# Softmax chunk totals summed over keys by VectorE in the FFN instead of by TensorE: a transformer block on one core

## The chip, the cores and the metric

The kernel runs on one core of a Trainium2 chip. Its time is the time of one execution on the device in microseconds (us); smaller is better. The engines of the core are TensorE (PE in the rows; PEld its weight loads), VectorE (DVE), ScalarE (ACT), GpSimd (POOL) and SyncE (SP, which here only starts transfers). Each follows its own list of instructions in order, and they wait for each other by semaphores.

## The reference, cut to what matters

```python
# x (4096, 512); 16 heads of 32 dimensions; float32 throughout
q, k, v = split(x @ Wqkv, 3);  q, k = layernorm(q) * q_scale, layernorm(k) * k_scale
scores = (q / sqrt(32)) @ k.T, per head;  -inf where key > query      # causal
attn   = softmax(scores)                                             # exp / sum over keys
x = layernorm(x + (attn @ v) @ out_W)
# FFN of width 2048 with weights (int - 128) * scale
x = layernorm(x + (silu(x @ Wg.T) * (x @ Wu.T)) @ Wd.T)
```

The part that the change touches is the denominator of the softmax: for each head and query, the sum of the exponentials over all keys.

## The kernel before, in words

It has three stages: the projections with the layer norms of q and k (to about 330 us of the span), the attention (330 to 1475) and the output projection with the FFN (1475 to the end).

The attention takes the heads in four groups (`g`) of four. In a group the queries go in eight chunks (`ch`) of 512, and the keys in blocks (`kb`) of 128. A pair (chunk, key block) is a step `t`; chunk `ch` has 4(ch+1) steps, so a group has 144, and `place(t)` is a step's place in its chunk. The four key blocks on the diagonal alternate with the first full ones, so they fill places 0, 2, 4 and 6. A step does this:

- PE: `scores` makes four tiles of 128 keys x 512 queries (one per head, two heads for each unit `u`) in PSUM banks, of which there are six (`BANKS`); a tile waits until ScalarE has read the tile that was in its bank before.
- ACT: the exponential of each tile, to `probs`, a ring of six steps (`PB`). It waits until the step that had the buffer before is used up, by PE (`valued`) and by whoever adds it (`added`, `side_added`).
- POOL: `mask` sets the wrong side of a diagonal block to zero.
- PE: `weigh` multiplies the four heads' probabilities by the values, side by side in four groups of 32 columns, into one PSUM bank `ctx_acc`.
- DVE: adds the step's 128x2048 probabilities to `total[:, ch % 2]`, keys still on the partitions.

The order of PE's work is written out by `scored_before`: inside a chunk (the run) six tiles of scores, one `weigh`, six tiles, two `weigh`; near a chunk's ends (four places at its start, three at its end) four tiles and one `weigh` in turn, with one batch of eight tiles where the run ends.

The sums over keys leave DVE in three ways. In chunks 4, 5 and 6 (`QUEUED`) every fourth step is added by a transfer instead: POOL starts a DMA that accumulates the step's `probs` into `side` (12 steps a group), and DVE adds `side` to `total` once, three steps before the chunk's end (`fold_at`). Five steps a group (`pe_sums`, one in chunk 3 and four in chunk 7) are added by PE, which multiplies them by a matrix of ones into the bank `sums_acc` (L1092). And each chunk's `total` is summed over its 128 keys by PE with the same ones (`sum_total`, L852), three steps into the next chunk; DVE copies `sums_acc` out (L1195), SP stores it, and reciprocals are taken of small tiles.

`finish` is the third stage. It takes the queries again in chunks of 512; each chunk has 16 positions ("ic", i), in which PE makes gate and up for 128 of the 2048 (`gate_up`) and adds the one before to the output (`down`), ACT takes the silu, and DVE forms the product in two parts (`make_hidden`), with the norms, the residuals (`"o"`), the transposes (`"t"`) and `context` between. Buffers `xt_hi` and `xt_lo` hold the transposed input of this chunk and, from the "t" positions on, of the next.

## Time and profile before

| what | value |
|---|---|
| median of 3 runs | 2299.28 us (2298.51 to 2304.28) |
| the profiled execution's own time | 2299.23 us |
| its span, first to last instruction | 2297.4 us |
| PE busy / DVE busy / ACT busy over the span | 99% / 76% / 59% |
| granted clock of PE over the span | 0.995 |
| mean DMA rate | 108 GB/s |

The span is divided between stages with different limits, so the shares over the whole say little of one stage. In the rows, "busy" counts time covered by at least one instruction; matmuls and exponentials overlap in their pipelines, so the spacing of their starts says more than their durations.

### The profile page before, as it was taken

The numbers are of one execution on the slowest core, as the hardware profiler recorded it, in microseconds if no ns is written. First come the engines' busy times: TensorE is split into PE (matmuls) and PEld (weight loads), VectorE is DVE, ScalarE is ACT, GpSimd is POOL, SyncE is SP. The second block draws the span as 40 slices with busy tenths as digits, with TensorE's granted clock in tenths as the row PEclk, the third lists the DMA queues.
The fourth block names the chain that finished last, engine by engine and source line by source line (L and its number), as shares of the span: only waits on it lengthen the run. The fifth ranks groups of instructions, "written<-read, shape, count | busy, mean of one in ns | idle before, by whom it ended". The sixth has DMA issues, their size and how long they took to land.

```text
span 2297.4 us, 35243 instructions
## 1 busy us (share of the span) xinstructions
PE 2270.1 (99%) x12422; PEld 1423.2 (62%) x12422; DVE 1746.0 (76%) x1796; ACT 1360.0 (59%) x2790; POOL 299.0 (13%) x323
## 2 busy tenths in 40 slices
PE   9999999999999999999999999999999999999997
PEld 7888854444444444444444444488888888888886
DVE  7777769999899998989989899945655556565554
ACT  4444479999999999999999999611111111101111
POOL 2111112211112111221111211000000000000001
PEclk9999989999999999999999999999999999999999
DMA  7768893443914438144391444531102111010100
GB/s 262 260 240 283 275 245 85 123 102 79 183 39 116 104 80 176 43 110 99 82 180 43 108 108 111 193 101 36 56 19 74 38 37 47 29 56 19 37 19 20
DMA packets 133221, 247.89 MB, mean 108 GB/s; under 512 B 15256, under 2 KB 40344, under 8 KB 126880
## 3 DMA queue, kind: packets, MB, share of 16 engines
q1 hardware_dynamic: 125840, 194.72, 30.6%
q0 software_dynamic: 6912, 50.33, 9.5%
q8 instruction: 101, 1.65, 0.3%
q14 instruction: 80, 0.66, 0.1%
q10 hardware_dynamic: 288, 0.52, 0.1%
HBM read 122.83 MB, written 72.37 MB: 85 GB/s over the span
## 4 chain that ended last, share of the span: by engine, by line
PE 83%; DVE 2%; ACT 1%; issue 0%; ACTq 0%; DVEq 0%; POOL 0%; POOLq 0%
PE score L1069 25%; PE ctx_acc L1084 22%; PE slot L1502 20%; PE y L1513 10%; PE slot L1427 3%; PE sums_acc L852 1%; ACT probs L1148 1%; DVE total L1210 1%; PE sums_acc L1092 1%; PE slot L1470 1%; PE y L1427 0%; PE slot L1494 0%; DVE stats L1599 0%; DVE x_late L1744 0%; ACT ctx_out L1133 0%
## 5 line engine op out<-in xcount | busy, mean ns | idle before, releaser
L1148 ACT ACTIVATE probs<-score 128x512 f32<-128x512 f32 (+3 forms) x2304 | 1068.5, 630 | 79.6 <-PE score L1069 69.2
L1210 DVE TENSOR_TENSOR total<-total,probs 128x2048 f32<-128x2048 f32 (+3 forms) x444 | 931.5, 2098 | 84.2 <-ACT probs L1148 35.0
L1069 PEld LDWEIGHTS score<-queries,keys 98*128 98x128 f32 x2300 | 392.7, 189 | 410.3 <-ACT probs L1148 325.9
L1069 PE MATMUL score<-queries,keys 98*128 98x512 f32 (+3 forms) x2300 | 630.6, 404 | 3.3 <-ACTq L1128 3.1
L1578 ACT ACTIVATE hidden<-slot,gate_scale_sb 128x512 f32<-128x512 f32 x128 | 88.2, 689 | 631.9 <-PE slot L1502 628.5
L1084 PE MATMUL ctx_acc<-probs,values 128*32 128x512 f32 (+3 forms) x3584 | 420.9, 561 | 0.0
L1640 DVE SCALAR_TENSOR_TENSOR hidden<-slot,up_scale_sb,hidden 128x512 f32<-128x512 f32 x128 | 96.1, 751 | 252.8 <-ACT hidden L1578 252.8
L1012 POOL TENSOR_SCALAR_AFFINE_SELECT probs<-probs 128x512 f32<-128x512 f32 x128 | 178.9, 1398 | 645.2 <-ACT probs L1148 644.8
L1502 PE MATMUL slot<-xt_hi,w_front 128*128 128x512 f32 x600 | 233.6, 389 | 0.1
L1502 PE MATMUL slot<-xt_lo,w_front 128*128 128x512 f32 x600 | 233.5, 389 | 0.0
L1084 PEld LDWEIGHTS ctx_acc<-probs,values 128*32 128x32 f32 x3584 | 85.4, 108 | 186.5 <-issue 98.3
L1502 PE MATMUL slot<-xt_hi,w_back 128*128 128x512 f32 x416 | 163.2, 392 | 0.0
L1502 PE MATMUL slot<-xt_lo,w_back 128*128 128x512 f32 x416 | 162.0, 389 | 0.0
L433 PE MATMUL score<-w_hi,x_hi 128*128 128x512 f32 x384 | 156.3, 407 | 1.0 <-DVE w_lo L615 0.9
L433 PE MATMUL score<-w_hi,x_lo 128*128 128x512 f32 x384 | 150.4, 392 | 0.0
L433 PE MATMUL score<-w_lo,x_hi 128*128 128x512 f32 x384 | 149.9, 390 | 0.0
L1084 PE MATMUL ctx_acc<-probs,first_values 128*32 128x512 f32 (+3 forms) x1024 | 132.9, 591 | 0.7 <-ACT ctx_out L1133 0.7
L1389 POOL TENSOR_TENSOR rstd<-veps,minus_half 128x1 f32<-128x1 f32 x64 | 36.5, 570 | 716.2 <-DVE veps L1604 716.2
L1502 PEld LDWEIGHTS slot<-xt_hi,w_front 128*128 128x128 f32 x600 | 112.6, 188 | 23.9 <-DVE hidden L1640 0.5
L1502 PEld LDWEIGHTS slot<-xt_lo,w_front 128*128 128x128 f32 x600 | 112.6, 188 | 23.4
L1513 PE MATMUL y<-w_front,h_hi 128*128 128x512 f32 x288 | 112.0, 389 | 0.0
L1513 PE MATMUL y<-w_front,h_lo 128*128 128x512 f32 x288 | 112.0, 389 | 0.0
(152 smaller groups left out, 2252.3 us busy)
## 6 DMA issues: line engine op xcount, KB each, us to landing
side<-probs POOLq DMA_DIRECT2D x48, 1024.0 KB, 6.9
queries<-q_hi SPq DMA_DIRECT2D x64, 256.0 KB
keys<-k_hi SPq DMA_DIRECT2D x64, 256.0 KB
wq_int<-in_wq SPq DMA_DIRECT2D x48, 256.0 KB, 3.3
wq_float<-wq_f SPq DMA_DIRECT2D x48, 256.0 KB, 2.9
x_raw<-in_x_t SPq DMA_DIRECT2D x32, 256.0 KB, 4.2
k_lo<-part_lo SPq DMA_DIRECT2D x32, 256.0 KB, 2.4
queries<-q_lo SPq DMA_DIRECT2D x32, 256.0 KB
```

What stands on the lines that cost most here:

```text
L433: ins = pe.matmul(bank[:], x[:, par, dc, rows], w[:, dc, m * D:(m + 1) * D], start=dc == 0 and a == 0, stop=dc == DC - 1 and a == 2)
L1012: pool.affine_select(out=view, in_=view, compare_op=ALU.is_ge, fill=0.0, base=0, pattern=[[0, HG], [1, P]], channel_multiplier=-1).then_in ...
L1069: pe.matmul(bank(v)[:, cut(t):], keys[0:ROWS, kb // ST, h, kb % ST * P:(kb % ST + 1) * P], queries[0:ROWS, q_buffer[ch], h, cut(t):], star ...
L1084: ins = pe.matmul(ctx[h * HD:(h + 1) * HD, n0:], value(kb)[:, h * HD:(h + 1) * HD], probs[:, t % PB, h, n0:], start=t in first, stop=t in ...
L1148: act.activation(probs[:, t % PB, h, cut(t):], bank(v)[:, cut(t):], ACT.Exp).then_inc(exped, 1)
L1210: dve.tensor_tensor(into, into, now, ALU.add).then_inc(added, 1)
L1389: pool.tensor_tensor(rstd[:, k, st:st + 1], veps[:, k, st:st + 1], minus_half[:], ALU.pow).then_inc(rooted[k], 1)
L1427: ins = pe.matmul(bank[:], a[:, h, g, q * P:(q + 1) * P], w[:, g, :], start=first, stop=g == NG - 1 and a is cp_lo)
L1502: ins = pe.matmul(slot[pos % 2][q][:], v(w[:, dc * P:(dc + 1) * P]), v(x[:, par, dc, :]), start=dc == 0 and a == 0, stop=dc == DC - 1 and ...
L1513: ins = pe.matmul(y[st][:], v(x[:, st * P:(st + 1) * P]), v(tile(i, 2)), start=i == 0 and a == 0, stop=i == IC - 1 and a == 1)
L1578: act.activation(hidden[:, i % 2, :], slot[pos % 2][0][:], ACT.Silu, scale=gate_scale[:, i:i + 1]).then_inc(gated, 1)
L1640: dve.scalar_tensor_tensor(hid, slot[pos % 2][1][:], up_scale[:, i:i + 1], hid, ALU.mult, ALU.mult)\
```

## The change

- No sums on PE: `sum_total`, the five `pe_sums` steps, the bank `sums_acc`, DVE's `take_sums` and the small stores and reciprocals are gone.
- `QUEUED` is now (3, 4, 5, 6, 7): 2 + 3 + 4 + 5 + 6 = 20 steps a group go by accumulating transfer, into two side buffers (`sides`, by the chunk's parity), and 124 steps by DVE.
- DVE's fold is gone. POOL starts a transfer instead that accumulates `total` into the side buffer (`fold`), four steps into the next chunk.
- Each chunk's totals, 1 MB a chunk and group (128 keys x 4 heads x 512 queries), are stored to DRAM by SP (`store_total`), from `total` for chunks 0 to 2 and from the side buffer for chunks 3 to 7; chunk 0's twice.
- The sum over keys is made later by DVE: the totals come back with the queries on the partitions (`piece_load`, runs of 256 bytes) and `tensor_reduce` sums over keys. For chunks 0 and 1 this is done in the last group of the attention, 16 pieces of 16 keys (512 KB each), one every five steps from step 46; for chunks 2 to 7 (and an unused copy of chunk 0) in the FFN, four pieces of 32 keys (1 MB each) for each of seven chunks.
- The freed PSUM bank is a seventh bank of scores.
- SP's transfers are issued in an order written out by steps; three of the next group's eight key loads now start inside chunk 7.

```diff
-    BANKS = 6
-    PE_SUMS = 5
-    QUEUED = (4, 5, 6)
+    BANKS = 7
+    QUEUED = (3, 4, 5, 6, 7)
+    FOLD_LAG, SIDE_LAG = 4, 8
+    PIECE_FROM, PIECE_EVERY, PIECE_LAG = 6, 5, 3
...
+    piece_at = [first[QUEUED[1]] + PIECE_FROM + PIECE_EVERY * p for p in range(2 * PIECES)]
...
-                if by_pe(t):
...
-                        ins = pe.matmul(sums[h * HD:(h + 1) * HD, n0:], ones[:], probs[:, t % PB, h, n0:],
-                                        start=opens, stop=False)
...
-                    if t - TOTAL_LAG in last:
-                        sum_total(pe, g, last.index(t - TOTAL_LAG))
...
+        def wait_total_free(engine, g, ch):
+
+            if ch >= 2:
+                before, gb = ch - 2, g
+            else:
+                before, gb = NCH + ch - 2, g - 1
+            if gb < 0:
+                return
+            if before in QUEUED:
+                engine.wait_ge(folded, 16 * (NF * gb + folds_before(before) + 1))
+            else:
+                engine.wait_ge(total_stored[ch % 2], total_stores(gb, before))
...
+            def fold(g, ch):
+
+                pool.wait_ge(added, NA * g + adds_before(last[ch] + 1) + A_CREDIT)
+                pool.wait_ge(side_added, 16 * (NQ * g + queued_before(last[ch])))
...
+                pool.dma_start(sides[ch % 2][:], total[:, ch % 2, :, :], accum_op=ALU.add).then_inc(folded, 16)
...
                         elif place(t) == 1:
 
 
-                            dve.wait_ge(totaled, NCH * g + ch + 1)
+                            wait_total_free(dve, g, ch)
...
-                    if t in fold_at:
-                        dve.wait_ge(side_added, 16 * (NQ * g + queued_before(last[ch])))
...
+                    if g == NG - 1 and t in piece_at:
+                        reduce_piece(piece_at.index(t))
...
+            def reduce_piece(n, par, p):
+
+                dve.wait_ge(piece_in[p % 2], 16 * NG * (LATE_PIECES // 2 * n + p // 2 + 1))
+                dve.tensor_reduce(part[:, p, :], piece_room(1 - par, p).rearrange("p k q -> p q k"), AX.X, ALU.add).then_inc(reduced, 1)
...
+                        reduce_in = (5, 6, 11, 12) if before else (1, 2, 11, 12)
+                        if after and i in reduce_in:
+                            reduce_piece(n, par, reduce_in.index(i))
```

Where instructions stand before and after, at the three places that matter:

PE in the first group before: the one step of chunk 3 that goes to the sums (731), the batch of eight tiles where that chunk's run ends (736), and the sum of chunk 3's total after the third step of chunk 4 (746):

```order
730 L1084 MATMUL ctx_acc<-probs,values 32x512 x4
731 L1092 MATMUL sums_acc<-probs,ones 32x512 x4
732 L1069 MATMUL score<-queries,keys 128x512 x6
...
736 L1069 MATMUL score<-queries,keys 128x512 x8
737 L1084 MATMUL ctx_acc<-probs,values 32x512 x4
...
745 L1084 MATMUL ctx_acc<-probs,values 32x384 x4
746 L852 MATMUL sums_acc<-total,ones 32x512 x4
747 L1069 MATMUL score<-queries,keys 128x128 x4
```

and the end of chunk 3 after (the tiles of a batch stand in several rows, since the seventh bank has a name of its own):

```order
727 L1135 MATMUL score<-queries,keys 128x512 x3
728 L1135 MATMUL score_spare<-queries,keys 128x512
729 L1135 MATMUL score<-queries,keys 128x512 x6
730 L1150 MATMUL ctx_acc<-probs,values 32x512 x4
...
742 L1150 MATMUL ctx_acc<-probs,values 32x384 x4
743 L1135 MATMUL score<-queries,keys 128x128 x4
```

Both groups of `sums_acc` are gone and nothing else of PE's has moved; the batch at the run's end is in three rows.

POOL after, from chunk 7 of the first group over the start of the second (AFFINE_SELECT is `mask`; x5 is the four steps of chunk 0 and the first of chunk 1):

```order
59 L1078 DMA side_odd<-probs 128x2048 [waits side_stored1,exped]
60 L1063 AFFINE_SELECT probs<-probs 128x4x128 [waits exped]
61 L1080 DMA side_odd<-probs 128x2048 [waits side_added,exped] x5
62 L1063 AFFINE_SELECT probs<-probs 128x4x128 [waits exped] x5
63 L1089 DMA side_odd<-total 128x2048 [waits folded,added,side_added]
64 L1063 AFFINE_SELECT probs<-probs 128x4x128 [waits exped] x10
```

and DVE's adds at the start of the second group after (chunk 0, then chunk 1 from the third row on):

```order
394 L1275 TENSOR_TENSOR total<-probs 128x4x384 [waits masked,folded,exped]
395 L1270 TENSOR_TENSOR total<-total,probs 128x4x256 [waits added,masked,exped]
396 L1270 TENSOR_TENSOR total<-total,probs 128x4x128 [waits added,masked,exped]
397 L1275 TENSOR_TENSOR total<-probs 128x2048 [waits masked,folded,exped]
398 L1270 TENSOR_TENSOR total<-total,probs 128x4x384 [waits added,masked,exped]
```

The first add of chunk 1 (397) needs the buffer that chunk 7 used, and so the transfer of POOL's row 63; before, it waited for `sum_total`.

SP after, in the last group, in chunk 6 (L144 stores the product of chunk 5, L941 its side buffer, L151 loads a piece):

```order
747 L144 DMA ctx<-ctx_out 128x512 [waits ctx_taken]
748 L151 DMA piece<-totals 32x16x64 [waits reduced]
749 L151 DMA piece<-totals 32x16x64 x3
750 L941 DMA totals<-side_odd 128x2048 [waits folded]
751 L151 DMA piece<-totals 32x16x64 [waits reduced]
752 L151 DMA piece<-totals 32x16x64 x3
```

The piece that DVE needs at place 12 of the chunk (751) stands in line behind the side buffer's store (750), which waits for POOL's fold; it is so in chunks 4, 5 and 6. Before, this line held neither.

## Rows read from the trace of the kernel before

**Rows 1.** The page: each engine's busy time, its share of the span, and instructions.
```profile
PE 2270.1 (99%) x12422; PEld 1423.2 (62%) x12422; DVE 1746.0 (76%) x1796; ACT 1360.0 (59%) x2790; POOL 299.0 (13%) x323
```
**Rows 2.** Stretches (second group, last group, FFN): length, busy us, clock, DMA share.
```profile
618.00:907.00 289.00, 288.73 (x1833) 127.45 (x1832) 263.77 (x133) 269.90 (x585) 53.09 (x44) 1.00 0.47 104
...
1196.00:1475.00 279.00, 278.37 (x1764) 121.78 (x1762) 256.91 (x127) 259.55 (x558) 50.13 (x39) 1.00 0.42 109
...
1560.00:2200.00 640.00, 639.94 (x2870) 528.84 (x2870) 365.58 (x644) 98.36 (x156) 27.39 (x50) 1.00 0.13 39
```
**Rows 3.** The page's chain that ended last, by engine and line.
```profile
PE score L1069 25%; PE ctx_acc L1084 22%; PE slot L1502 20%; PE y L1513 10%; PE slot L1427 3%; PE sums_acc L852 1%; ACT probs L1148 1%; DVE total L1210 1%; PE sums_acc L1092 1%; PE slot L1470 1%; PE y L1427 0%; PE slot L1494 0%; DVE stats L1599 0%; DVE x_late L1744 0%; ACT ctx_out L1133 0%
```
**Rows 4.** Waits from 330 to 1500: us in total, times, longest.
```profile
ACT probs L1148 <- PE score L1069: 65.5, 85, 1.4
...
ACT probs L1148 <- DVE total L1210: 3.1, 2, 1.7
```
**Rows 5.** Timeline of PE in chunk 7's run: start, us, what.
```profile
852.08 1.06 PE L1084 MATMUL ctx_acc<-probs,values 128*32 128x512 f32 x8
853.07 1.66 PE L1069 MATMUL score<-queries,keys 98*128 98x512 f32 x6
...
864.13 1.06 PE L1084 MATMUL ctx_acc<-probs,values 128*32 128x512 f32 x8
865.01 1.04 PE L1092 MATMUL sums_acc<-probs,ones 128*32 128x512 f32 x8
865.98 0.50 PE L1069 MATMUL score<-queries,keys 98*128 98x512 f32 x1
```
**Rows 6.** Timeline of PE where the run of chunk 6 ends.
```profile
824.03 1.66 PE L1069 MATMUL score<-queries,keys 98*128 98x512 f32 x6
825.62 1.07 PE L1084 MATMUL ctx_acc<-probs,values 128*32 128x512 f32 x8
826.62 2.52 PE L1069 MATMUL score<-queries,keys 98*128 98x512 f32 x8
829.07 1.06 PE L1084 MATMUL ctx_acc<-probs,values 128*32 128x512 f32 x8
```
**Rows 7.** Timeline of ACT in the same run.
```profile
799.67 32.63 ACT L1148 ACTIVATE probs<-score 128x512 f32<-128x512 f32 x65
```
**Rows 8.** Instructions of DVE by shape, second group: busy us, mean ns | idle before.
```profile
L1210 DVE TENSOR_TENSOR total<-total,probs 128x2048 f32<-128x2048 f32 x88 | 204.5, 2324 | 16.0 <-ACT probs L1148 8.0
...
L1195 DVE COPY sums_out<-sums_acc 128x512 f32<-128x512 f32 x8 | 5.5, 684 | 2.1 <-PE sums_acc L852 2.1
```
**Rows 9.** Instructions of DVE by shape, 0 to 330: reductions.
```profile
L659 DVE TENSOR_REDUCE whole<-wq_f 128x512 f32 x36 | 24.4, 676 | 0.0
```
**Rows 10.** The tile `side`: POOL's issues, and its transfers' time to landing.
```profile
L1028 POOL DMA_DIRECT2D side<-probs x36: 838/855/907, 415.6 to 1394.9; - x36
...
DMA to landing us min/median/max: 4.4/6.9/8.7
```
**Rows 11.** DMA issues: count, KB each, median us to landing.
```profile
w_front<-wq_float SPq DMA_DIRECT2D x7, 1024.0 KB, 5.7
...
x_late<-sums SPq DMA_DIRECT2D x1, 224.0 KB, 2.8
```
**Rows 12.** Timelines of POOL and ACT where the third group starts.
```profile
903.57 0.63 POOL L1012 TENSOR_SCALAR_AFFINE_SELECT probs<-probs 128x512 f32<-128x512 f32 x1 [1.96 <-ACT probs L1148]
...
913.54 0.78 ACT L1148 ACTIVATE probs<-score 128x128 f32<-128x128 f32 x4 [0.54 <-PE score L1069]
```
**Rows 13.** Timelines of DVE and ACT where the attention ends.
```profile
1461.12 14.27 DVE L1210 TENSOR_TENSOR total<-total,probs 128x2048 f32<-128x2048 f32 x6
...
1461.83 10.56 ACT L1148 ACTIVATE probs<-score 128x512 f32<-128x512 f32 x21
```
**Rows 14.** Timeline of DVE in the FFN, positions 6 and 12 of a chunk.
```profile
1630.33 0.75 DVE L1640 SCALAR_TENSOR_TENSOR hidden<-slot,up_scale_sb,hidden 128x512 f32<-128x512 f32 x1 [3.04 <-ACT hidden L1578]
...
1674.18 0.75 DVE L1640 SCALAR_TENSOR_TENSOR hidden<-slot,up_scale_sb,hidden 128x512 f32<-128x512 f32 x1 [2.58 <-ACT hidden L1578]
```

More of the change, by code:

```diff
@@ L843, in attend, with bank @@
         g_full = probs[:, 0, 2, 0:P]
-        def sum_total(pe, g, ch):
-            opens = not any(by_pe(x) for x in range(first[ch], last[ch] + 1))
-            if opens:
-                pe.wait_ge(sums_taken, NCH * g + ch + 1)
-            pe.wait_ge(added, NA * g + adds_before(last[ch] + 1) + A_CREDIT)
-            for h in range(HG):
-                ins = pe.matmul(sums[h * HD:(h + 1) * HD, :], ones[:], total[:, ch % 2, h, :], start=opens, stop=True)
-            ins.then_inc(totaled, 1)
-        def bank(v):
-            return score[v % BANKS // 2][:, v % 2, :]
+        def bank(g, v):
+            b = (HG * NS * g + v) % BANKS
+            return spare if b == BANKS - 1 else score[b // 2][:, b % 2, :]
+        def wait_total_free(engine, g, ch):
[9 more added lines that the diff above has]
+                engine.wait_ge(total_stored[ch % 2], total_stores(gb, before))
         def value(kb):
@@ L1085, in weigh, with group @@
                                     probs[:, t % PB, h, n0:], start=t in first, stop=t in last)
[L1086 to L1093 removed]
                 ins.then_inc(valued, 1)
[L1096 removed]
+            def group(g, after):
                 done = early
```

371 lines of the change are left out of this document (213 added, 158 removed).

## The prediction

> **What bounds the kernel now.** I read the page first, then tables by stretch, and then the chain, the waits and timelines inside a group. The page has PE busy for 99% of the span and the other engines much less [rows 1], and the chain of work that ended last is PE's in attention and FFN alike, with the sums at 1% and 1% [rows 3]. By stretch the picture splits. In the FFN PE is busy for 639.94 of 640 us and DVE for 365.58. In an attention group of 289 us, though, ACT is busy for 269.9 and DVE for 263.8 [rows 2]: three engines within 10%, so work taken from PE pays only until the next one is in the way.
>
> "Busy" covers overlapping matmuls, so the question is what PE waits for. In the run, PE's pattern takes three steps: a lone `weigh` starts at 852.08 and the one of the pattern after next at 864.13, so a pattern takes 6.02 us [rows 5]. ACT does 65 exponentials in 32.63 us without a gap that the view shows, 0.502 each, which is also 6.02 us for twelve [rows 7]. Two engines at one pace: one follows. All ACT waits in the attention come to 65.5 us for PE's scores and 3.1 for DVE [rows 4]. ACT waits for PE and next to nothing else, so PE leads. The 65.5 us is also a ceiling: PE can become faster by about that before ACT stands in its place.
>
> **The sums on PE.** Per group of four heads: eight `sum_total` and five steps, 13; in four groups 52. One costs this: `weigh` to the next score is 853.07 - 852.08 = 0.99 us; with the sums between it is 865.98 - 864.13 = 1.85 [rows 5]. Net 0.86. The last two (the step 143 of the last group, and chunk 7's total) stand behind the last `weigh`, where the head of the next stage waits for DVE anyway, so 50 count: 50 x 0.86 = 43.0 us. Nothing hides them; each moves PE's next scores, for which ACT waits. Of the 65.5 us they use two thirds. **-43.0**.
>
> **The seventh bank.** In the run six tiles take 825.62 - 824.03 = 1.59 us, so eight at that pace would take 2.12; the batch of eight took 829.07 - 826.62 = 2.45 [rows 6]. So 0.33 us is lost where tiles seven and eight wait for ACT to free a bank. One more bank lets PE go on one exponential (0.502) earlier, which covers it. Chunks 2 to 7 have such an end: 24 in all, 0 to 24 x 0.33 = 8 us. Batches of six never need the seventh. I take 0.3 each, since ACT may be what bounds the steps just behind. **-7**.
>
> **DVE's adds.** Per group three adds, three folds and eight copies go: 6 x 2.3 + 5.5 = 19.3 us of DVE's 263.8 [rows 2, 8]. That is room, not time; DVE held ACT up for 3.1 us in all.
>
> **The head.** Six adds without a gap end at 1475.39, when ACT had been done since 1472.39 [rows 13], and the next stage's first work on DVE stands behind them. Step 143 was PE's; now DVE has one add more, 2.3 us, partly made up since its backlog at step 138 is smaller. **+1.5** (0 to 2.4).
>
> **The fold at a group's start.** The first add of chunk 1 used to wait for `sum_total`; now it waits for POOL's transfer of chunk 7's total, issued after the mask of chunk 1's first step. That mask ends at 903.57 + 0.63 = 904.20. With landings as those of `side`, 6.9 us from the issue [rows 10, 12], the total is free at 911.1, the add (2.3) ends at 913.4. Behind it ACT waits: step 10 writes the buffer of step 4, which it did at 913.54 [rows 12], and by 912.7 once the sums between are gone. So 0.7 us is lost without contention. But SP stores chunk 0's total at that time, twice (2 MB; 1 MB took 5.7 us to land [rows 11]), on the same DMA engines: up to 5 us more. It happens three times: 0 to 3 x 6 = 18. I take 2.5 each, nearer to the row without contention. **+7.5**.
>
> **The pieces in the last group.** 16 reductions of 16 x 64 = 1024 elements: a reduction of 512 takes 0.676 [rows 9], so one of 1024 about 1.2, 19 us together, and some 2 for the rest. DVE in that group: 256.9 - 19.3 + 21 = 258.6 of 279 - 11 = 268 [rows 2]: 96%, and in the runs of chunks 4 to 7 nearly all, since three adds in four steps are 3 x 2.36 = 7.1 and a piece every five steps adds 1.0 per four, together the 8.03 that four steps take. No room for late pieces there, and three are late: SP may issue them only behind the side buffer's store, which waits for the fold (issued after place 4, landed 6.9 us later, at place 8 to 9); then 1 MB (5.7) and 512 KB in runs of 256 bytes (224 KB took 2.8 us, so 6.4 at most [rows 11]) land at place 11.5 to 14, for use at 11 or 12. DVE stalls 2 to 4 us each, which ACT feels where its six buffers are used up. **+6** (0 to 25).
>
> A rule of the Trainium skill bears on how such transfers share the engines. Each DMA engine, it says, takes turns between queues at whole packets of some 9 to 17 descriptors (DMA: Bandwidth & Descriptors, section on queues, rings and completion order). By it an accumulating transfer would hold back a piece for its whole length, and pieces would land at the late end; by [rows 10, 11] alone they could as well share. No row here has the two together. The sum by the rule would be some 5 us larger.
>
> **More transfers.** 20 steps a group go by transfer in place of 12, and five folds; the time to landing must stay below what six buffers give. A buffer comes back five steps (10.0 us) after its exponentials; POOL's issue is 0.86 and landing 6.9, 8.7 at worst [rows 10]: up to 9.6. Key loads now run beside them in chunk 7, so I take **+1** (0 to 10).
>
> **The FFN.** Four reductions of 2048 elements a chunk, each (by 0.676 for 512, less a fixed part) about 2.3 us, and a small end. They stand behind `make_hidden` at positions 5, 6, 11, 12, where DVE then idles for 3.04 and 2.58 us [rows 14] (and more at 6 and 12). They fit, the tightest by 0.3. The pieces (2 MB, 6 x 2 x 2 = 24 us at the most by the same row) have five positions of 5.4 us and more. DMA share there is 0.13 [rows 2]. **0**.
>
> Sum: -43.0 - 7 + 1.5 + 7.5 + 6 + 1 = -34.0. The profiled execution took 2299.23 us, 1.8 more than its span and the same as the median of the runs. 2299.2 - 34.0 = **2265 us**.
>
> **The rivals.** (a) *All is hidden*: the fold does not collide, pieces are in time, the bank gives its 8: 2299 - 43 - 8 + 1 = 2249. For it: DVE's fresh room and a mean DMA share of 0.47. (b) *DVE becomes the bound where it reduces*: the reductions read with a step of 64 elements, which no instruction in this trace does. If they take twice the row's price, the last group gets 17 us more on an engine with 9 free, +8 to the sum above, and in the FFN 4.6 us against idle of 3.04 and 2.58 leaves some 2 us a chunk, 7 x 2 = 14: 2287. The Trainium skill speaks for it: SBUF is read in lines of 16 bytes, and strides that leave the line at each element pay a penalty (SBUF — State Buffer, under the DMA port swizzle); it gives no price. (c) *ACT takes over*: PE and ACT have the same 6.02 us pace, and if ACT's own limit is near that, only what lies at the chunks' edges is gained: 32 x 0.86 = 27 less the losses of 16: 2288. Against it: exponentials at 0.502 include the waits in [rows 4]. (d) *The side transfers are late*, the one that ends slower: an aside that lands 9.2 us or more after its issue holds ACT at the buffer. There are 80 of them; 0.5 us each is 40 and cancels the gain, 1 us each gives 2299 - 34 + 80 = 2345. It decides from a mean landing of 9.7 us, 2.8 over today's; the longest now is 8.7.
>
> **How the numbers follow.** A measurement of this kernel can tell 0.3%, 7 us, from no change. Forecast (2256 to 2276) 0.42; (a) 0.20; (b) 0.13; (c) 0.12; (d) 0.07, half of it slower than before by more than 7 us; other mixtures 0.06, on the slow side of 2276 and half of them within 7 us. The range 2246 to 2290 leaves out (d), most mixtures and the ends of (a). Faster: 0.91; same 0.04; slower 0.05.
>
> **What would show it.** A group of 278 to 281 us instead of 289; run pattern still 6.02 us (if less, PE was following ACT: (c) in reverse); batches of eight at 2.1. DVE's first add of chunk 1 waiting for a DMA for 5 us or more, and ACT for that add, three times; waits of DVE for pieces at place 11 or 12 only in the last group. (b) shows in the duration of the reductions, (d) in `side` landing above 9 us and ACT waiting for a DMA. PE must stay busy for all of 1560 to 2160; any wait of gate and up for `make_hidden` refutes my zero.

## The result and the profile after

| | before | after |
|---|---|---|
| median, us | 2299.11 (4 runs, 2298.51 to 2304.28) | 2382.14 (4 runs, 2374.78 to 2382.79) |
| ratio of the medians | | 1.0349, 95% interval 1.0323 to 1.0374 |
| span of the profiled execution | 2297.4 us | 2381.0 us |
| granted clock over the span | 0.995 | 0.971 |

The change makes the kernel 3.5% slower. The forecast was 1.5% faster, and its range (2246 to 2290) missed. In what follows, a side transfer is one of POOL's accumulating transfers of a step's `probs` into a side buffer (1 MB). These are lines of the page of the kernel after, the engines and then the two DMA queues that matter (q1 is fed by SyncE, q0 by POOL's side transfers and folds):

```profile
PE 2276.3 (96%) x12006; PEld 1422.7 (60%) x12006; DVE 1814.5 (76%) x1797; ACT 1357.1 (57%) x2789; POOL 337.7 (14%) x375
...
q1 hardware_dynamic: 279360, 269.74, 44.9%
q0 software_dynamic: 14400, 104.86, 19.8%
```

PE was busy for 99% [rows 1] and is for 96% of a longer span: it now waits for something. Stretches, columns as in [rows 2]:

```profile
330.00:400.00 70.00, 50.35 (x320) 22.48 (x318) 41.91 (x22) 45.27 (x107) 13.70 (x12) 0.83 0.74 189
700.00:1000.00 300.00, 289.62 (x1751) 127.56 (x1750) 250.55 (x120) 270.84 (x590) 64.09 (x58) 0.97 0.73 177
1300.00:1560.00 260.00, 231.13 (x1282) 97.54 (x1281) 223.41 (x115) 205.92 (x431) 42.40 (x41) 0.94 0.84 192
1660.00:2285.00 625.00, 624.12 (x2792) 514.40 (x2791) 452.98 (x667) 98.04 (x156) 26.41 (x48) 1.00 0.46 82
```

In the attention the transfer engines' share rose from 0.42 to 0.47 to 0.73 to 0.84, and no compute engine fills these stretches. In the FFN PE is still busy throughout. The waits from 330 to 1560 (total, times, longest) name the new owners:

```profile
ACT probs L1201 <- PE score L1135: 46.2, 48, 3.0
ACT probs L1201 <- DMA side_odd<-probs: 34.5, 10, 6.7
ACT probs L1201 <- DVE total L1275: 32.9, 4, 21.1
DVE total L1275 <- DMA side_odd<-total: 26.4, 3, 9.1
DVE total L1275 <- DMA totals<-total: 24.9, 1, 24.9
DVE part L1248 <- DMA piece<-totals: 23.8, 6, 7.0
```

Beside [rows 4]: the wait for PE's scores fell from 65.5 to 46.2 (50.4 with the seventh bank's tiles, which have a name of their own), as forecast; the other five lines are waits for transfers, or ACT's for a DVE add that had waited for one.

**Where the time is.** ACT copies each chunk's result out once, so the spacing of these copies is a chunk's duration. Of the second group's chunk 7, after and before:

```profile
857.91 0.78 ACT L1186 ACTIVATE ctx_out<-ctx_acc 128x512 f32<-128x512 f32 x1
931.45 0.69 ACT L1186 ACTIVATE ctx_out<-ctx_acc 128x512 f32<-128x512 f32 x1
```
```profile
832.11 0.68 ACT L1133 ACTIVATE ctx_out<-ctx_acc 128x512 f32<-128x512 f32 x1
899.01 0.60 ACT L1133 ACTIVATE ctx_out<-ctx_acc 128x512 f32<-128x512 f32 x1 [1.04 <-PE sums_acc L1092]
```

73.5 us against 66.9. All chunks of the profiled execution, read in this way (us; g0 to g3 are the groups, the last column is chunk 0 of the next group):

| | ch1 | ch2 | ch3 | ch4 | ch5 | ch6 | ch7 | ch0 |
|---|---|---|---|---|---|---|---|---|
| before, each group (last: ch7 64.2) | 15.4 | 23.6 | 32.5 | 39.6 | 47.8 | 55.8 | 66.9 | 7.6 |
| after, g0 | 14.4 | **44.9** | 30.8 | 41.4 | 49.7 | 54.4 | **72.5** | 7.3 |
| after, g1 | **19.8** | 22.5 | 31.2 | 39.4 | 46.7 | 55.2 | **73.5** | 7.3 |
| after, g2 | **20.7** | 22.5 | 31.7 | 38.3 | 46.5 | 54.4 | **73.4** | 7.3 |
| after, g3 | **19.9** | 22.5 | 31.1 | **43.3** | **54.2** | **63.0** | **86.0** | |
| undisturbed (the best seen) | 14.4 | 22.5 | 31.0 | 38.3 | 46.5 | 54.4 | 61.9 | 7.3 |

From the last copy to the end: 823.0 before, 827.5 after. The last row (its 61.9 is from e3 below) sums to 276.3 against 289.2: the wanted gain is there where nothing disturbs, 12.9 us a group, some 51 in all, against my 43 + 7. What outweighs it, counted against the undisturbed row: g0's chunk 2, 22.4; chunk 1 of g1 to g3, 17.2; chunk 7 of g0 to g2, 33.7; chunks 4 to 6 of g3, 21.3; its chunk 7, 26.8 (against 64.2 - 5.0); the end, 4.5; small ones, about 9. Together 135 less 51 is 84, the difference of the spans.

### The profile page after: what moved, and what is told of

It is laid out like the page before. It is cut to its first block and busy times, and to the rows that moved or that the text cites. A ratio compares the mean times of both kernels' runs of the same rounds, so it can differ in the third digit from the quotient of the medians.

```text
span 2381.0 us, 34948 instructions
## 1 busy us (share of the span) xinstructions
PE 2276.3 (96%) x12006; PEld 1422.7 (60%) x12006; DVE 1814.5 (76%) x1797; ACT 1357.1 (57%) x2789; POOL 337.7 (14%) x375
## 3 DMA queue, kind: packets, MB, share of 16 engines
q1 hardware_dynamic: 279360, 269.74, 44.9%
q0 software_dynamic: 14400, 104.86, 19.8%
## 5 line engine op out<-in xcount | busy, mean ns | idle before, releaser
L1201 ACT ACTIVATE probs<-score 128x512 f32<-128x512 f32 (+3 forms) x1975 | 980.1, 667 | 149.3 <-PE score L1135 44.1
L1270 DVE TENSOR_TENSOR total<-total,probs 128x2048 f32<-128x2048 f32 (+3 forms) x432 | 906.9, 2099 | 132.4 <-ACT probs L1201 85.8
L1135 PE MATMUL score<-queries,keys 98*128 98x512 f32 (+3 forms) x1971 | 601.9, 411 | 66.7 <-ACT probs L1201 63.6
L1135 PEld LDWEIGHTS score<-queries,keys 98*128 98x128 f32 x1971 | 350.2, 193 | 434.3 <-ACT probs L1201 361.9
L1150 PE MATMUL ctx_acc<-probs,values 128*32 128x512 f32 (+3 forms) x3584 | 435.1, 578 | 7.9 <-ACT ctx_out L1186 4.6
L1201 ACT ACTIVATE probs<-score_spare 128x512 f32<-128x512 f32 (+3 forms) x329 | 221.0, 672 | 14.3 <-PE score_spare L1135 5.6
L1150 PE MATMUL ctx_acc<-probs,first_values 128*32 128x512 f32 (+3 forms) x1024 | 138.0, 612 | 1.8 <-POOL probs L1063 1.8
L1135 PE MATMUL score_spare<-queries,keys 98*128 98x512 f32 (+3 forms) x329 | 135.9, 413 | 3.7 <-ACT probs L1201 3.6
```

The lines of the kernel that those rows point to most:

```text
L1135: pe.matmul(bank(g, v)[:, cut(t):], keys[0:ROWS, kb // ST, h, kb % ST * P:(kb % ST + 1) * P], queries[0:ROWS, q_buffer[ch], h, cut(t):], s ...
L1150: ins = pe.matmul(ctx[h * HD:(h + 1) * HD, n0:], value(kb)[:, h * HD:(h + 1) * HD], probs[:, t % PB, h, n0:], start=t in first, stop=t in ...
L1201: act.activation(probs[:, t % PB, h, cut(t):], bank(g, v)[:, cut(t):], ACT.Exp).then_inc(exped, 1)
L1270: dve.tensor_tensor(into, into, now, ALU.add).then_inc(added, 1)
```

## The experiments

Each ran with the kernel before on the same chip (2298.9 to 2301.9). "After" is 2382.1, and its own four executions lie 8 us apart, so a difference of a few us from it shows little by itself; there the chunks of the profile say where it lies.

**e1: the first loads spread.** In group 0, one load of keys and values goes ahead and the others stepwise, as in the later groups.

```diff
-            for j in range(AHEAD, NCH):
-                load_kv(0, j)
+            load_kv(0, AHEAD)
...
-                    if g and at == 3 and ch in (1, 2, 3):
+                    if at == 3 and ch in (1, 2, 3):
...
-                    if g and at == 7 and ch == 2:
+                    if at == 7 and ch == 2:
```

> Edit: in group 0 the key and value loads of chunks 4 to 7 are issued step by step as in the other groups, not all at once ahead of everything. Theory T (named transfers come late because of what stands ahead of them at that place): the store of chunk 0's totals is no longer behind 5 MB of loads, DVE's one wait of 24.9 us for it goes, chunk 2 of group 0 takes 23 us instead of 44.9, total 2382 - 21 = 2361 (2355 to 2366). Rival U (the DMA engines as a whole are too full, share 0.73 against 0.47, and any relief is lost again elsewhere): 2373 or more. Rival C (the stall costs most through TensorE's clock, which falls to 0.5 after it): 2350 or less, since the low-clock stretch behind the stall goes too.

2358.8, ratio 1.0256 (1.0239 to 1.0273), 23.3 less; g0's chunk 2 took 22.5, and chunks 3 and 4, where loads now run, 3.3 and 1.0 more. The time is in theory T's range. The stall in the kernel after, from a timeline of SP, DVE and ACT:

```profile
343.97 1.08 SPq L99 DMA_DIRECT2D values<-v_rows  x1
...
352.67 1.99 SPq L947 DMA_DIRECT2D totals<-total  x2
...
367.23 2.29 DVE L1275 TENSOR_TENSOR total<-probs 128x2048 f32<-128x2048 f32 x1 [24.86 <-DMA totals<-total]
369.60 0.79 ACT L1201 ACTIVATE probs<-score 128x128 f32<-128x128 f32 x4 [21.06 <-DVE total L1275]
```

Chunk 2's first add needs the buffer whose total is being stored. SP comes to the store only behind five loads, at 352.67, and it lands 14 us later behind their data. I had weighed this wait for chunks 7 to 1, where a fold holds the buffer, and never for chunks 0 to 2, where a store does.

**e2: the fold earlier**, at step 1 of the next group instead of 4.

```diff
-                    elif g and t == FOLD_LAG:
+                    elif g and t == 1:
```

> Edit: at a group's start GpSimd issues the fold of chunk 7 behind step 1's mask instead of step 4's. Theory T: it lands three steps (5.7 us) sooner, DVE's three waits of 9 us before the first add of chunk 1 fall to about 3, chunk 1 takes 15 to 16 us instead of 20, total 2382 - 13 = 2369 (2364 to 2374). Rival U: the fold meets the key and query loads of the group's start and lands as late as before, 2378 or more.

2373.75, 1.0322 (1.0304 to 1.0339), 8.4 less; chunk 1 took 17.7, 16.3 and 18.0. At the slow end of the theory: of the 17.2 us over the undisturbed chunk, half went with the earlier issue. DVE's three waits for the fold still came to 19.6 us, 6.8 at most, in place of 26.4; that the other transfers there are what keeps them long is argued, not shown.

**e3: without the next group's first loads in chunk 7.**

```diff
+                if g and j < AHEAD:
+                    sp.sem_inc(k_in[j], 48)
+                    sp.wait_ge(valued, NS * g + end + V_CREDIT)
+                    sp.sem_inc(v_in[j], 16)
+                    return
                 key_load(sp, dr, keep, g, j, k_in[j])
```

> Leaves out: the key and value loads of the next group's first three chunks (1 MB each, issued inside chunk 7), so groups 1 to 3 compute on group 0's keys there. Theory T: the accumulating transfers of chunk 7 start late because of these loads; without them chunk 7 of groups 0 to 2 takes 62 to 64 us instead of 73, total 2382 - 30 = 2352 (2345 to 2360), and side transfers land in about 7 us with none over 9. Rival U: the engines stay at a share above 0.65 and chunk 7 stays above 69 us, 2372 or more.

2345.3, 1.0208 (1.019 to 1.0225), 36.8 less, the largest single piece. Chunk 7 took 62.7, 61.9, 61.9, and ACT's wait for side transfers fell from 34.5 us to this (with the other buffer's, from 37.0 to 13.9):

```profile
ACT probs L1206 <- DMA side_odd<-probs: 8.3, 5, 3.2
```

In the kernel after, the place looks like this (POOL and SP in the second group's chunk 7):

```profile
883.51 0.65 SPq L76 DMA_DIRECT2D keys<-k_hi  x1
886.40 0.85 POOL L1080 DMA_DIRECT2D side_odd<-probs  x1 [12.06 <-DMA side_odd<-probs]
...
899.97 0.84 POOL L1080 DMA_DIRECT2D side_odd<-probs  x1 [12.71 <-DMA side_odd<-probs]
```

POOL waits 12 us for the side transfer before it may issue the next. The view of the tile gives 13.0 us from the issue at 886.40 to the landing, and 7.2 for the one at 899.97, beside which no load is issued. Undisturbed, two side transfers are issued four steps apart, 8.0 us; as each waits for the one before, a landing later than that also delays the next.

**e4 and e5: the pieces.** e4 leaves out loads and reductions of chunks 0 and 1 in the last group, e5 the reductions alone.

```diff
# e4
-                piece_load(sp, dr, piece[:], n, slice(k * PIECE_KEYS, (k + 1) * PIECE_KEYS), piece_in)
+                sp.sem_inc(piece_in, 16 * NG)
# e4, e5
-                dve.tensor_reduce(part[:, k, :], piece[:].rearrange("p k q -> p q k"), AX.X, ALU.add).then_inc(reduced, 1)
+                dve.sem_inc(reduced, 1)
```

> Leaves out: the sum over keys of chunks 0 and 1 in the last group, both the 16 loads of 512 KB in runs of 256 bytes and VectorE's 16 reductions (the inverses of these chunks are stored as ones). Theory T: chunks 4 to 7 of the last group take what they take in groups 1 and 2, or less where those have key loads: 39, 47, 55 and 64 us instead of 43, 54, 63 and 86, total 2382 - 41 = 2341 (2333 to 2350). Rival U: 20 us or more of that loss stays, from the accumulating transfers and weight loads alone, 2360 or more.

> Leaves out the 16 reductions of the pieces of chunks 0 and 1 in the last group (and the small sum and reciprocal behind them; ones are stored as their inverses), but keeps all loads of the pieces and DVE's waits for them. Theory D (VectorE's time is the cost: 16 reductions of 1.99 us and the small ones, about 34 us, on an engine that has about 9 us free in that group): the time is near that of the kernel that leaves out loads and reductions, 2350 to 2360. Rival Q (the transfers are the cost: 8 MB of pieces in runs of 256 bytes beside the side transfers, which then land late): most of the 29 us stays, 2370 to 2380.

e4: 2353.4, 1.0238 (1.0221 to 1.0255), 28.8 less, where 41 was expected; chunks 4 to 7 of the last group took 39.4, 50.2, 54.4, 76.7. e5: 2366.45, 1.0292 (1.0274 to 1.0311), 15.7 less; 41.7, 52.6, 59.0, 77.9. Neither pure theory: DVE's time is 16 us and the loads 13. And chunk 7 stays 17.5 us over the undisturbed 59.2 without any piece, so something else disturbs it.

**e10: the same reductions, read in order.**

```diff
-piece[:].rearrange("p k q -> p q k")
+piece[:].rearrange("p k q -> p (k q)").rearrange("p (q k) -> p q k", q=QB)
```

> The 16 reductions of 1024 elements in the last group and the 28 of 2048 in the FFN read the same tiles and as many elements, but in runs of neighbouring elements, so that they sum the wrong ones; loads and waits are unchanged. Theory S (the step of 64 elements between reads is what doubles the reduction's time): 1024 elements take 1.15 to 1.25 us in place of 1.99 and 2048 take 2.3 to 2.4 in place of 3.8; VectorE gets 13 us back in the last group and the time comes down by 5 to 10 us there and up to 3 in the FFN: 2370 to 2378. Rival (a reduction is this slow for its count of elements or outputs, whatever the order): durations and time unchanged.

2369.1, 1.0299 (1.028 to 1.0319), 13.1 less. By shape (columns as in [rows 8]), the kernel after and then this one:

```profile
L1732 DVE TENSOR_REDUCE part<-xt_hi 128x64 f32<-128x2048 f32 x14 | 53.5, 3820 | 0.0
...
L1248 DVE TENSOR_REDUCE part<-piece 128x64 f32<-128x1024 f32 x16 | 31.6, 1976 | 23.8 <-DMA piece<-totals 23.8
```
```profile
L1732 DVE TENSOR_REDUCE part<-xt_hi 128x64 f32<-128x2048 f32 x14 | 31.9, 2278 | 0.0
...
L1248 DVE TENSOR_REDUCE part<-piece 128x64 f32<-128x1024 f32 x16 | 19.4, 1215 | 29.8 <-DMA piece<-totals 29.8
```

The step of 64 elements costs 63% to 68%. In order, both sizes are what [rows 9] gives (1.2 and 2.3 us, my figures). SBUF is read in lines of 16 bytes and each access that crosses to a new line pays a penalty, says the Trainium skill (SBUF — State Buffer, under the DMA port swizzle); these rows agree. The 13.1 us are more than the reductions give: in the profiled executions the last group's chunks 4 to 7 took 5.1 less and the end 2.5 less, and the rest is scattered over places without a reduction. In the FFN, DVE waits for nothing new, and PE loses under 1 us of 625: my zero holds there, though its reason (2.3 us each) did not.

**e6: the last group's weights behind the side transfers.** ctx and x loads at place 27 of chunk 7, weight loads behind them.

```diff
-                        if ch == NCH - 1 and at == 3:
-                            wait_scored(NG - 1, last[NCH - 2] + 1)
+                        if ch == NCH - 1 and at == 27:
+                            wait_scored(NG - 1, t)
...
+            wait_scored(NG - 1, last[NCH - 1] - 3)
             for j in range(FRONT):
```

> Nothing is left out. In the last group's chunk 7 the loads of the context and of x (place 3) and the seven loads of the FFN's first weights are issued behind the last side transfer, from place 27 on. Theory W (the loads beside the side transfers make these late, as the key and value loads do in groups 0 to 2): chunk 7 of the last group comes from 86.0 to about 75 us, the time to 2366 to 2374. Rival V (that chunk is long because VectorE, with the reductions, is behind; the loads only use idle queues): 2378 to 2384, or the stall moves to the head of the next stage, which then waits for its weights.

2377.7, 1.0343 (1.0324 to 1.0363), only 4.5 less. Chunk 7 came down from 86.0 to 71.4, more than expected, but from there to the end it takes 841.2 instead of 827.5: the loads cost 14 us on either side of the border, as rival V has it in its second form. So these loads are what still disturbed e4's chunk 7 (e7 below, without pieces and with late weights, takes 62.6 there).

**e7 and e8: all out, with seven and with six banks.** The edits of e1 to e4 and e6 together; e8 with `BANKS = 6`.

> The four edits measured so far together (key and value loads of group 0 spread, fold at step 1, without the next group's first three key and value loads inside chunk 7, without pieces of chunks 0 and 1 in the last group) and the late weights. It leaves out those loads and reductions. If the losses are separate and what remains is the forecast's gain (no sums on TensorE, seventh bank), the time is 2382 - 23.4 - 8.4 - 36.8 - 28.8 = 2285, and about 10 less by the late weights: 2270 to 2287. Rival: they cover each other, or ScalarE is next in the way once TensorE waits for no transfer (rival c of the forecast): 2290 to 2305.

> As the kernel of all five edits, with six banks of scores in place of seven (same leaving out). The difference of the two is the seventh bank's worth where nothing else stalls. Forecast's term: 24 ends of runs at 0.3 us, so 5 to 8 us slower than with seven. Rival: ScalarE bounds the steps just behind, and the bank is worth nothing: within 1 us of it. Other rival: six banks are also worse inside the run, where a batch of six tiles then waits for the last exponential: more than 12 us.

e7: 2296.4, 0.998 (0.997 to 0.9989). e8: 2302.3, 1.0012 (1.0 to 1.0024). The bank is worth 5.9 us, where I had 7. The rest fell: 2296 is at the rival's end. But not because ACT took over: its waits for scores came to 19.3 us and the chunk table shows 54.4 for chunk 6 and 61.8 to 62.7 for chunk 7 in every group. The end takes 840.7, 17.7 more than before, for the late weights (see e6) and the head (e11), and some 30 more against the undisturbed row are spread over chunks (42.2 and 49.9 in g0's chunks 4 and 5, where its last loads now run; 18.0 in g3's chunk 1). Even with these loads and reductions left out, the change is worth 4 us beside the kernel before (2300.4).

**e11: the wanted part alone.** The kernel before without its sums on TensorE.

```diff
-                if by_pe(t):
+                if False:
...
+            if g or ch:
+                pe.sem_inc(totaled, 1)
+                return
```

> The kernel before, without its sums on TensorE: the 20 steps of sums and 31 of the 32 totals' sums are left out (one stays, so that the bank is written), so its denominators are wrong; waits, copies, stores, side transfers, loads and six banks stay. It measures the term of -43.0 (50 times 0.86) alone. If that term is right: 2299 - 43 = 2256, within 2253 to 2262. Rival (TensorE was followed so closely by ScalarE and VectorE that they take over): 2270 or more, with ScalarE or VectorE waited for in the run.

2272.8, 0.9877 (0.9861 to 0.9894): 29.1 less, not 43: outside the term's range, and on the rival's side of 2270. ACT's wait for scores fell from 65.5 to 32.2 us, so PE still led it on the whole. The chunks that hold sums gain as forecast: chunk 3 takes 30.8 (two sums, -1.7), 4 and 6 -0.8 and -0.9, chunk 7 62.6 (five, -4.3). Chunks 0 and 1, with a total's sum each, gain 0.5 and next to nothing. Chunk 5 in three groups has a stall of up to 1.5. And the end takes 828.2 us instead of 823.0. That is the head (the start of the next stage), by timelines of DVE and PE and by the stretch:

```profile
1429.14 14.27 DVE L1213 TENSOR_TENSOR total<-total,probs 128x2048 f32<-128x2048 f32 x6
...
1445.46 0.80 PE L1430 MATMUL y<-ow_hi,cp_hi 128*128 128x512 f32 x1 [7.35 <-DVE cp_lo L1701]
1446.90 0.63 PE L1430 MATMUL y<-ow_hi,cp_hi 128*128 128x512 f32 x1
```
```profile
1438.00:1448.00 10.00, 2.65 (x10) 2.07 (x7) 9.60 (x11) 3.22 (x6) 1.05 (x2) 0.65 0.20 79
...
1446.00:1451.00 5.00, 5.00 (x13) 3.90 (x12) 2.52 (x7) 1.75 (x3) 0.00 (x0) 0.50 0.14 54
```

PE finishes earlier, but DVE's backlog is six adds without a gap, as before, and the head stands behind it. PE waits 7.35 us where it waited 0.93 and 1.08 before, its granted clock falls to the 1.2 GHz level (0.50 from 1446 to 1451), and a product takes 0.63 us in place of 0.39 until 1451. This is separate from transfers, and my term of +1.5 for the head missed it.

**e9 and e12: loads moved in SP's program.**

```diff
-                            if t == key_end[j] + 1:
-                                load_kv(g + 1, j)
+                        if ch == NCH - 1 and at in (15, 27, 30):
+                            load_kv(g + 1, (15, 27, 30).index(at))
...
-                        load_kv(g, {1: 4, 2: 5, 3: 7}[ch])
+                    for j, when in {3: (1, 6), 4: (2, 3), 5: (2, 8), 6: (3, 3), 7: (3, 10)}.items():
# e12
-                dve.tensor_reduce(part[:, k, :], piece[:].rearrange("p k q -> p q k"), AX.X, ALU.add).then_inc(reduced, 1)
+                    dve.tensor_tensor(running[:], running[:], piece[:], ALU.add).then_inc(reduced, 1)
```

> Nothing is left out. Group 0's key and value loads are spread, the fold of chunk 7 goes out at step 1, and the next group's first three key and value loads go out at places 15, 27 and 30 of chunk 7 (in place of about 8, 12 and 16), its loads 3 to 7 in chunks 1 to 3 away from the folds. Theory K (the losses come from where the loads stand beside the side transfers): 2382 - 23 - 8 and 20 to 30 of the 37 us that leaving these loads out gave: 2321 to 2331. Rival: the transfer engines have no quiet place left in these groups, moving gives back elsewhere what it saves: 2345 or more.

> Nothing is left out. As the kernel with the moved loads, and in addition the pieces of chunks 0 and 1 are added up in a running tile of 16 x 64 (contiguous adds of 1024 elements, about 1.2 us each, in place of reductions of 1.99), with one strided reduction per chunk at the end, and the last four of the seven loads of the FFN's first weights go out behind the last side transfer. VectorE has 12 us less in the last group. Expected 8 to 14 us below the kernel with the moved loads. Rival: the late weights cost at the head what they save in chunk 7, and only the adds count: 4 to 8.

e9: 2371.2, 1.0295 (1.0278 to 1.0312). e12: 2370.7, 1.0295 (1.0277 to 1.0312). Both misses, and e9 does not test what it was meant to: SP waits for a free buffer, not for a place, so the "moved" loads were issued at the same time as ever, and chunk 7 stayed at 72 to 73. What it did move was two loads into chunk 3, beside its side transfers: chunk 3 then took 37.1 to 39.2 in place of 31, some 7 us a group. e12's cheaper adds (1.32 us) gave next to nothing: the last group's chunks 4 to 7 took 245.2 us in place of 246.7. As e12 also moves weight loads, it does not show why.

**e13, e14, e15: loads held until a side transfer has landed**, by a real wait. e14 holds the weights too and keeps e12's running tile; e15 is e14 without pieces.

```diff
-                            if t == key_end[j] + 1:
+                        if ch == NCH - 1 and at in (12, 16, 20):
+                            sp.wait_ge(side_added, 16 * (NQ * g + queued_before(t)))
...
+                        if ch == NCH - 1 and at in (16, 20, 24, 28):
+                            j = at // 4 - 4
+                            sp.wait_ge(side_added, 16 * (NQ * g + queued_before(t)))
+                            weight_load(sp, dr, keep, keep["w_front"][:, j * ST:(j + 1) * ST, :], j)
```

> Nothing is left out. Group 0's loads spread, fold at step 1, and each of the next group's first three key and value loads in chunk 7 now waits until the side transfer of place 9, 13 or 17 has landed, so that it falls into the gap before the next one (a side transfer moves data for 5.2 of every 8 us). Theory O (overlap is the cost: a load in front of a side transfer delays its start to 4 to 6 us after the issue and stretches it to 7.4): chunk 7 of groups 0 to 2 comes from 73 to 63 to 66 us, the time to 2382 - 23 - 8 - 25 = 2326, within 2320 to 2335. Rival B (volume: 1 MB does not fit the gap of 2.8 us, the engines are full either way): chunk 7 stays above 70, 2345 or more.

> Nothing is left out. As the kernel with held loads, and in the last group too: the context and x loads wait for the side transfer of place 5, the first four of the FFN's weight loads for those of places 13, 17, 21 and 25, and the pieces are added up in a running tile with contiguous adds (1.32 us in place of 1.99). Theory O: the last group's chunk 7 comes from 86 to 74 or less, 10 to 16 us below the kernel with held loads, 2310 to 2316. Rival B: within 5 us of it.

> As the kernel with held loads and held weights, and leaving out the pieces of chunks 0 and 1 in the last group, loads and reductions both (ones are stored as the inverses). It bounds what any cheaper way of summing those two chunks could give. Theory O: the last group's chunks 4 to 7 at 39, 48, 54.5 and 64 us, 2326 - 29 - 12 = 2285. Rival B: chunk 7 at 76 as without held weights, 2297 or more.

e13: 2348.1, 1.0207 (1.0189 to 1.0224). e14: 2350.7, 1.0215 (1.0198 to 1.0232). e15: 2335.0, 1.0154 (1.0136 to 1.0171). Chunk 7 took 72.6, 71.7, 72.0 in e13, and 80.1 and 75.1 in the last group of e14 and e15, so rival B forecast the times. But theory O was not tested, for there was no gap (SP and POOL in e13's second group):

```profile
855.59 0.34 SPq L76 DMA_DIRECT2D keys<-k_hi  x1
856.08 0.85 POOL L1079 DMA_DIRECT2D side_odd<-probs  x1 [8.30 <-DMA side_odd<-probs]
...
866.22 0.31 SPq L76 DMA_DIRECT2D keys<-k_hi  x1
...
866.71 0.84 POOL L1079 DMA_DIRECT2D side_odd<-probs  x1 [9.78 <-DMA side_odd<-probs]
```

The side transfer issued at 846.92 took 8.6 us to land, longer than the 8.0 between two. So POOL's next side transfer waited for the same landing as the load, and the load went out 0.5 us in front of it; that one then took 10.1 us, and the same happened at 866 and 878. e13's gain over e1 (10.7) is in chunk 1.

**e16, e17, e18: in the kernel before.** e16 makes only its five sums into side transfers (20 a group); e18 releases the loads behind the next side transfer's issue; e17 leaves 19 side transfers and one sum, with the loads behind the last of them.

```diff
-    PE_SUMS = 5
-    QUEUED = (4, 5, 6)
+    PE_SUMS = 0
+    QUEUED = (3, 4, 5, 6, 7)
...
+                    for j in range(AHEAD):
+                        sp.wait_ge(side_added, 16 * (NQ * before + queued_before(first[NCH - 1] + 12 + 4 * j)))
+                        load("kv", j)
# e18
+                        sp.wait_ge(issued, NQ * before + queued_before(first[NCH - 1] + 12 + 4 * j))
# e17
+    pe_sums = {first[NCH - 1] + 25}
...
+                        sp.wait_ge(side_added, 16 * (NQ * before + queued_before(last[NCH - 1])))
```

> The kernel before with one part of the change alone, nothing left out: the five steps a group that TensorE summed go by side transfer (chunks 3 to 7, 20 steps, still one side buffer, folded by VectorE), the next group's first three loads held behind side transfers in chunk 7, its others behind the stores of chunks 0 to 3, and the first four weight loads held in the last group. The chunk totals are still summed by TensorE, six banks, no totals to DRAM, no pieces. TensorE has 20 sums less, 17 us. Theory O: 2282 to 2290, a version faster than both. Rival B: side transfers in chunk 7 cost what they do after the change, about 6 us a group, and it is 2300 or more.

> As the kernel before with side transfers in place of the five sums (2340.7), nothing left out, but each of the next group's first three loads, and the first four weight loads in the last group, waits until POOL has issued the side transfer of place 9, 13, 17 (13 to 25 for the weights), so it stands behind it and not in front. Theory F (standing in front is the cost, since a side transfer begins only when loads issued before it have moved): side transfers begin 1.4 us after their issue again, chunk 7 comes from 77 to 63 to 67 us, the time to 2284 to 2300. Rival B (volume): each side transfer takes 7.2 us of data instead, lands late all the same, and chunk 7 stays above 72, 2320 or more.

> The kernel before, nothing left out, with 19 side transfers a group in place of 12 (chunks 3 to 7, in chunk 7 at places 5, 9, 13, 17 and 21), one step a group summed by TensorE (place 25 of chunk 7) in place of five, and the next group's first three loads, as the last group's first four weight loads, held until the side transfer of place 21 has landed, so that none stands beside one. 16 sums of 0.86 us less: 2299 - 13.8 = 2286. If the first key load is late for the next group's scores, up to 2 us a group come back: 2285 to 2293. Rival: chunk 7 above 68 us a group from something that is not these loads (the query loads at its start, VectorE's 26 adds and a fold in 63 us): 2300 or more.

e16: 2340.7, 1.0171 (1.0151 to 1.019). e18: 2347.8, 1.0217 (1.0198 to 1.0236). e17: 2308.2, 1.0035 (1.0024 to 1.0046). Chunk 7 took 76.9 to 77.7 in e16, 77.3 to 78.2 in e18, and 68.9, 72.5, 68.9 in e17, against 66.9 with five sums. As in e13, each load that waits for a landing goes out 0.5 us in front of the side transfer that waits for the same one. One such collision in e16, with the wait that it makes:

```profile
868.67 0.32 SPq L76 DMA_DIRECT2D keys<-k_hi  x1
...
869.16 0.86 POOL L1033 DMA_DIRECT2D side<-probs  x1 [9.28 <-DMA side<-probs]
...
882.74 1.57 ACT L1153 ACTIVATE probs<-score 128x512 f32<-128x512 f32 x3 [5.99 <-DMA side<-probs]
883.14 0.85 POOL L1033 DMA_DIRECT2D side<-probs  x1 [13.12 <-DMA side<-probs]
```

It is 13.4 us from the issue at 869.16 to the landing, and 6.9 for the one at 906.43, which is alone. In e18 the load is issued 0.08 us behind the side transfer,

```profile
883.36 0.85 POOL L1034 DMA_DIRECT2D side<-probs  x1 [13.18 <-DMA side<-probs]
883.44 0.31 SPq L76 DMA_DIRECT2D keys<-k_hi  x1
```

and this one took 15.0 us. Theory F's time (2284 to 2300) is missed, but F itself is not refuted: e18 had loads in front too. Its first load, held up behind the queries, went out at 868.45, 0.9 us in front of the side transfer at 869.33, and SP's queue was still moving data when the one at 883.36 was issued. The queues' lines for 882.0 to 883.4 and for 883.4 to 889.0:

```profile
q1 hardware_dynamic: 412, 0.29, 119.6%
...
q1 hardware_dynamic: 963, 1.06, 109.9%
```

In the second stretch, 5.6 us behind the side transfer's issue, SP's queue moved 1.06 MB and POOL's nothing: the side transfer began only behind the load. (POOL's issue itself lasts 0.85 us; a load that waits for the transfer's first data was not tried.) e17 has none of these loads beside side transfers and its g3 takes 64.4; what is left (2 to 6 us a group in chunk 7) falls on the side transfers that stand beside the 1.5 MB of queries issued from 849 to 856: the one issued at 847.54 landed after 9.3 us and the one at 857.41 after 11.8, the others after 7.0 at most. By the price of 0.86, moving the five sums off PE alone would be worth 17 us, and the transfers that replace them cost 58 (e16, with its loads in front of side transfers) or, with one sum kept and nothing beside them but queries, 23 (e17).

## Why the prediction was wrong, step by step

- **The sums on PE, -43.0.** The price of 0.86 was right wherever a chunk is undisturbed, but 50 was not the count that pays: totals' sums in chunks 0 and 1 gave 0.5 and 0 (e11). e11 measured 29.1 in all; in its profiled execution the chunks gave 36 and the head took 5 back. That PE leads and ACT follows was right.
- **The seventh bank, -7.** 5.9 (e7 against e8).
- **The head, +1.5.** 5.2 in e11, and part of the 4.5 at the end in the kernel after, where PE waits 3.25 us for `cp_lo`. The step counted one add more; it left out that DVE's backlog stays when PE is done earlier.
- **The fold at a group's start, +7.5.** The mechanism was right, the size was off: 17.2 by the table, 5.4 to 6.3 each where I took 2.5. That is at the far end of my bounds (0 to 18): SP's transfers beside the fold cost what I had as "up to 5 us more".
- **The pieces, +6.** Measured 28.8 (e4), of which 15.7 is DVE's time (e5). Rival (b), which had twice the row's price, was the right one there: 1.98 us, not 1.2; its other half, 14 us in the FFN, did not come. My bound of 25 was short. The loads, which I took as late for DVE alone, also delay side transfers.
- **More transfers, +1, the step that failed.** It took `side`'s landing of 6.9, 8.7 at worst [rows 10], for the price of 32 more. Those rows come from chunks 4 to 6, in which no key, value or weight load runs; before, all of these run in chunk 7 and at its end, where there was no side transfer. The change puts six side transfers a group into just that chunk. It cost 33.7 us in three groups' chunk 7 (36.8 by e3), and some 17 in the last one's by the weights (e4, e6): about 51 us where I had 1 (0 to 10). Rival (d) had the mechanism and 9.2 us as its threshold, but as a mean over all 80. It is not: the 80 side transfers land after 8.5 us in the mean, 21 of them after more than 9.2, mostly one behind another. The step also had no term for the wait of each for the one before: a landing above 8.0 us puts off the next issue. The view of one of the two tiles:

```profile
DMA to landing us min/median/max: 4.9/7.7/14.0
```

- **No term at all: chunk 2 of group 0, 22.4** (23.3 by e1). I listed what each wait replaced only where a fold is involved; `wait_total_free` waits for a store in chunks 0 to 2, behind the group's first loads.
- **The FFN, 0.** Right to within a microsecond.

That the gain of the sums and the bank (-51 in the undisturbed row, against my -50) and the FFN came as forecast does not help the total, which has the wrong sign; and that row takes the best of every chunk, so its 51 is an upper bound of the gain. With these sizes, -51 (the undisturbed row) + 22 + 17 + 34 + 29 (e4) + 17 (what e4 left of chunk 7: 76.7 - 59.2) + 4 is 72; the small stalls of the table make 81 of the 84. Not settled: how a side transfer and a load share the engines. The Trainium skill says that an engine drains a whole packet of one queue before it turns to another (DMA: Bandwidth & Descriptors, section on queues, rings and completion order); the 5.6 us in e18 in which only SP's queue moved data speak against plain sharing and are in line with long turns, but no run here shows what ends such a stretch. Not tried either: loads in a real gap between side transfers. In e13, e14, e16 and e18 each stood beside one. No kernel tried here beats the one before on its full work.

## What to carry to other kernels

A price read from a row holds for the neighbourhood of that row. Before moving transfers, list for the new place which other transfers are issued there, from SP's timeline, and take the idle landing time only where there are none. When an instruction comes to wait for a buffer, ask for every use of the buffer which transfer frees it, and what stands in front of that transfer. Placing a transfer later in a queue's program moved nothing in e9, since it did not wait for anything that happens later. And when a load is to go into the gap behind a transfer, look at what else waits for that landing: in e13 it was the next transfer, and there was no gap.

## What the runs showed of the hardware

- A side transfer of 1 MB (accumulating, SBUF to SBUF) lands in 6.9 us alone. With 1 MB of keys and values issued around it, it took 10.1 to 11.4 us where the load went out 0.5 us in front (e13), 13.0 where three quarters of it were issued 4.4 to 2.2 us before (after, 886.40) and 13.4 and 15.0 where other data of SP's queue were in front too (e16, e18).
- A TENSOR_REDUCE with a step of 64 float32 elements takes 1.98 us for 1024 elements and 3.82 for 2048, in order 1.215 and 2.278.
- A stall cost more than its length: after PE's wait of 7.35 us its products took 0.63 us instead of 0.39 for 5 us, and over 330 to 400 us, around the stall of 21 us, the granted clock was 0.83.
